# The first block of a mixer in another order, and two residual sums in front of the last running product

## The chip, the cores and the metric

The kernel runs on one NeuronCore of one Trainium2 chip. Its engines each work through a queue of their own: TensorE (PE, matrix products into PSUM), VectorE (DVE), ScalarE (ACT), GpSimd (POOL) and SyncE (SP, which issues DMAs). They wait for one another by counting semaphores. The metric is the device time of one execution in microseconds (us), lower is better.

## The reference

One decoder layer on `x` of 8 x 256 tokens with 256 channels, in three residual steps: a gated state-space mixer, a causal attention with 16 heads on a second input, and a mixture of 8 experts. The change is in the mixer:

```python
x = _lin(x, w1)
x = _depthwise_conv(x, conv_w, conv_b)
x = jax.nn.silu(x)
x_delta = jax.nn.softplus(_lin(x, dl_w, dl_b))
A_t = _lin(x, A_w, A_b)
A_bar = jnp.exp(-x_delta * A_t)
B_x = _lin(x, B_w, B_b)
A_cum = jnp.cumprod(A_bar, axis=1)
h = jnp.cumsum(B_x * A_cum, axis=1)
ssm_out = _lin(h, C_w, C_b) + _lin(x, D_w, D_b)
x_res = jax.nn.silu(_lin(ssm_out, w2))
z = ssm_out * x_res
out = ssm_out + _lin(z, w3)
```

Its input is the layer norm of `x`, and `x + out` goes on to the attention, after another layer norm.

## The kernel before

**Blocks.** `mixer_and_projections` works on four blocks `i` of 512 tokens (NBLK = 4), channels on the 128 partitions in two halves `m` (DC = 2), the hidden 512 channels in four quarters (HC = 4). Every fp32 product is made of three fp32r products: each operand is split into a high part (a copy by ScalarE, `..._high`) and a low part (the difference, by VectorE or GpSimd, `..._low`), and `split_product` (L101) adds high x high, low x high and high x low. Weights are split so too: `high_weights` (ACT L623), `low_weights` (DVE L1040, POOL L554).

**A block's way.** Layer norm to `xn` (L1045 on VectorE for block 0, `normed` on ScalarE, L631, for the others, which needs `off1` from `offset`, DVE L1060), a turn by PE (`turn_x`, L838), `w1`, the convolution (`before_conv` on ScalarE, `conv` on VectorE, L1085 and L1087), tanh and silu (L651, L1092), high and low part of the result, `sh` and `sl` (ACT L657, DVE L1064 in block 0, afterwards POOL L568). PE then makes the chunks `dl`, `A`, `B` for the four quarters in a ring of four PSUM banks. Per quarter ScalarE takes exp (L666), log (L671) and exp (L676), VectorE `dmin` (L1097), `delta` (L1102, L1106), the running product `running` (a scan in two pieces, L1115) and `weighted` (L1122). ScalarE and GpSimd split the result into `gh` and `gl` (L683, L568). `mixed` (PE) multiplies it by C_w, `summed` (L1143) sums along the tokens. The gate and `w3` of block i - 1 run inside block i; `residual` (L1149) adds the product to `x_sb` in place, and the statistics of the next layer norm follow (L1054, then seven small steps L110 to L118, then `power` on GpSimd, L559).

**Other work in a block.** PE makes `keys`, `values` and, two blocks later, `queries` from the second input. `values(i)` waits for both residuals of block i - 1 (`x_out`). `mixed(i, m)` waits for the low part of the keys, `biased_low(i, "K")` on VectorE (L1164), which stands behind the statistics.

**Order.** All queues are written out by hand; nothing is scheduled. Each engine executes its queue in order, so a wait holds all that stands behind it. Constants and the statistics of blocks 1 to 3 for the first layer norm (`st1`) are put into gaps of the first block.

## Time and profile before

| | us |
|---|---|
| median of 3 runs | 716.22 |
| lowest, highest | 714.62, 717.73 |
| the profiled execution | 713.61 |
| its span | 711.8 |
| PE busy | 609.7 (86%) |
| DVE busy | 501.5 (70%) |
| ACT busy | 353.2 (50%) |
| POOL busy | 334.0 (47%) |

The span goes from the first to the last instruction. Shares are averages over stages: the mixer fills about the first 230 us, the attention and the experts the rest. The mean granted clock of TensorE is 0.926 of full speed; it takes two levels, 0.50 (1.2 GHz) and 1.00 (2.4 GHz).

### The profile page before, as it was taken

What the parts mean: (1) busy time and instruction counts of PE and PEld (TensorE: products, weight loads), DVE (VectorE), ACT (ScalarE), POOL (GpSimd) and SP (SyncE); (2) the same over time, 40 slices, a digit from 0 to 9 for tenths busy, and PEclk for the clock granted to TensorE, in tenths of its full rate; (3) what the DMA queues carried; (4) which work ended last, traced back from release to release, by engine and by line L of the source; (5) the groups of instructions that cost most, each with busy time, mean ns of one, the idle gap of its engine ahead of it and who ended that gap; (6) DMA issues with size and microseconds to landing.
All of it is one profiled execution on the core that took longest, in us unless ns stands there. A gap on an engine that the chain in (4) does not pass through costs nothing.

```text
span 711.8 us, 11906 instructions
## 1 busy us (share of the span) xinstructions
PE 609.7 (86%) x4100; PEld 507.7 (71%) x4100; DVE 501.5 (70%) x1066; ACT 353.2 (50%) x685; POOL 334.0 (47%) x322
## 2 busy tenths in 40 slices
PE   3596998998998789889897833999999999999992
PEld 2374877877876555456564522999999999999991
DVE  5777579689679956677776441687787878887740
ACT  4566472672452333354534311566666666666650
POOL 1224624223232003422453375446767868686776
PEclk9898999999999988999999755899999999999997
DMA  9300500873726944865673303505446252621223
GB/s 291 100 1 30 148 29 18 260 242 93 196 63 165 222 93 97 235 152 148 169 198 115 107 26 121 175 6 164 98 101 163 37 174 29 173 30 17 26 32 45
DMA packets 63315, 81.64 MB, mean 115 GB/s; under 512 B 10295, under 2 KB 47938, under 8 KB 63256
## 3 DMA queue, kind: packets, MB, share of 16 engines
q1 hardware_dynamic: 53928, 72.85, 36.4%
q0 software_dynamic: 9216, 7.81, 7.6%
q8 instruction: 33, 0.54, 0.3%
q10 hardware_dynamic: 112, 0.23, 0.1%
q14 instruction: 26, 0.21, 0.1%
HBM read 48.27 MB, written 34.36 MB: 116 GB/s over the span
## 4 chain that ended last, share of the span: by engine, by line
PE 40%; DVE 6%; DMA 5%; POOL 4%; issue 4%; ACT 2%; SPq 1%; POOLq 0%; DVEq 0%; ACTq 0%
PE l_scores L101 14%; PE l_turned L1857 7%; PE l_out L1857 3%; PE l_shared L1857 3%; DMA l_hi<-md 3%; POOL out L1561 2%; PE l_turned L337 2%; PE l_scores L1791 2%; PE l_shared L1733 2%; PE l_out L357 2%; DMA l_lo<-kd 1%; PE l_scores L1814 1%; PE l_turned L321 1%; DVE l_nm L291 1%; POOL disp L1530 1%
## 5 line engine op out<-in xcount | busy, mean ns | idle before, releaser
L2046 DVE SCALAR_TENSOR_TENSOR w_v<-w_th,l_scores 128x324 f32<-128x324 f32 x128 | 62.2, 491 | 56.5 <-ACT w_th L1648 56.0
L1648 ACT ACTIVATE w_th<-l_scores 128x324 f32<-128x324 f32 x128 | 56.5, 441 | 84.1 <-PE l_scores L101 83.3
L1548 POOL TENSOR_TENSOR l_lo<-w_v,l_hi 128x324 fp32r<-128x324 f32 x64 | 59.0, 922 | 75.6 <-ACT l_hi L1654 75.4
L367 ACT ACTIVATE l_area<-l_turned 128x1024 f32<-128x1024 f32 x48 | 49.1, 1023 | 88.6 <-PE l_turned L337 88.4
L101 PE MATMUL l_scores<-l_hi,w_w1h 128*128 128x324 f32 x256 | 81.4, 318 | 2.3 <-DVE l_lo L2038 1.1
L1561 POOL DMA_INDIRECT out<-l_area,w_to x48 | 76.3, 1591 | 12.2 <-issue 10.0
L101 PE MATMUL l_scores<-l_lo,w_w1h 128*128 128x324 f32 x256 | 80.8, 316 | 0.0
L101 PE MATMUL l_scores<-l_hi,w_w1l 128*128 128x324 f32 x256 | 80.7, 315 | 0.0
L291 DVE TENSOR_REDUCE l_nm<-l_scores 128x4 f32<-128x1024 f32 (+1 forms) x45 | 54.8, 1217 | 25.0 <-PE l_scores L277 24.8
L1654 ACT ACTIVATE l_hi<-w_v 128x324 fp32r<-128x324 f32 x128 | 59.9, 472 | 12.4 <-DVE w_v L2046 11.8
L2020 DVE TENSOR_TENSOR w_w2l<-w_s,w_w2h 128x256 fp32r<-128x256 f32 x56 | 60.2, 1075 | 1.9
L1537 POOL TENSOR_TENSOR w_w1l<-w_s,w_w1h 128x256 fp32r<-128x256 f32 x64 | 55.3, 864 | 1.7 <-ACT w_w1h L1633 0.2
L101 PEld LDWEIGHTS l_scores<-l_hi,w_w1h 128*128 128x128 f32 x256 | 49.2, 192 | 3.0 <-ACT l_hi L1643 2.9
L101 PEld LDWEIGHTS l_scores<-l_hi,w_w1l 128*128 128x128 f32 x256 | 49.4, 193 | 0.0
L101 PEld LDWEIGHTS l_scores<-l_lo,w_w1h 128*128 128x128 f32 x256 | 49.3, 193 | 0.0
L101 PE MATMUL l_scores<-m_sh,l_hi 128*128 128x512 f32 x96 | 39.5, 412 | 9.6 <-ACT m_sh L657 6.9
L1520 POOL TENSOR_TENSOR a_on<-a_po,a_rc 128x256 f32<-128x256 f32 x16 | 9.9, 620 | 73.5 <-DVE a_rc L1933 73.5
L568 POOL TENSOR_TENSOR m_gl<-m_acc,m_gh 128x512 fp32r<-128x512 f32 x16 | 24.5, 1533 | 37.4 <-ACT m_gh L683 37.4
L101 PE MATMUL l_scores<-m_sl,l_hi 128*128 128x512 f32 x96 | 38.8, 404 | 0.0
L101 PE MATMUL l_scores<-m_sh,l_lo 128*128 128x512 f32 x96 | 38.7, 403 | 0.0
L559 POOL TENSOR_TENSOR m_rstd<-m_ve,c_mhalf 128x4 f32<-128x4 f32 (+1 forms) x7 | 8.3, 1189 | 63.2 <-DVE m_ve L118 63.2
L1530 POOL DMA_INDIRECT disp<-w_x,w_si x32 | 31.7, 992 | 12.1 <-issue 8.2
(449 smaller groups left out, 1733.2 us busy)
## 6 DMA issues: line engine op xcount, KB each, us to landing
w_s<-in_L_ffn_w SPq DMA_DIRECT2D x14, 1024.0 KB, 6.4
l_lo<-kd SPq DMA_DIRECT2D x32, 200.0 KB
l_hi<-qd SPq DMA_DIRECT2D x32, 192.0 KB
disp<-c_blank SPq DMA_DIRECT2D x8, 658.1 KB
w_rows<-disp SPq DMA_DIRECT2D x7, 658.1 KB
kd<-l_qkh SPq DMA_DIRECT2D x16, 256.0 KB, 4.7
vd<-l_area SPq DMA_DIRECT2D x4, 1024.0 KB, 6.8
qd<-l_qkh SPq DMA_DIRECT2D x16, 256.0 KB, 4.4
```

Of the source, the lines that this page charges most:

```text
L101: mm = pe.matmul(out, a, b, start=first and n == 0, stop=last and n == 3 * len(parts) - 1)
L291: dve.tensor_reduce(dst, src, AX.X, ALU.max).then_inc(A["nm"], 1)
L367: act.activation(lead.pr[n % 3][:, :], lead.tbank[:, :], ACT.Exp, scale=SCALE).then_inc(A["exp"], 1)
L1530: pool.indirect_dma_start(out=disp, out_offset=bass.IndirectOffsetOnAxis(ap=si[:, k, t:t + 1], axis=0), in_=x3[:, t, :], in_offset=None, b ...
L1537: pool.tensor_tensor(w1_piece(w1l, f), w1_piece(s1[e % 2], f), w1_piece(w1h, f).bitcast(F32), ALU.subtract)\
L1548: pool.tensor_tensor(hl[:, g % 3, half(1)], v[:, n % 4, :], hh[:, g % 3, half(1)].bitcast(F32), ALU.subtract)\
L1561: pool.indirect_dma_start(out=out, out_offset=bass.IndirectOffsetOnAxis(ap=to[:, e % 3, t:t + 1], axis=0), in_=y[e % 2][:, t, :], in_offse ...
L1648: act.activation(th[:, n % 2, :], hb[n % 2][:, 0:HALF], ACT.Tanh, scale=0.5).then_inc(F["th"], 1)
L1654: act.activation(hh[:, g % 3, half(u)], v[:, n % 4, :], ACT.Copy).then_inc(F["hh"], 1)
L1857: mm = pe.matmul(eb[2 * k + u][:, 0:HALF], w2_piece(w, f)[:, k * P:(k + 1) * P], a[:, g % 3, half(q)], start=f == 0 and n == 0, stop=f == ...
L2020: dve.tensor_tensor(w2_piece(w2l, f), w2_piece(s2[e % 2], f), w2_piece(w2h, f).bitcast(F32), ALU.subtract)\
L2046: dve.scalar_tensor_tensor(v[:, n % 4, :], th[:, n % 2, :], 1.0, hb[n % 2][:, 0:HALF], ALU.add, ALU.mult).then_inc(F["v"], 1)
```

## The change

It has two parts. In the first block:

- PE makes the four products `dl` and `A` of quarters 0 and 1 together, `first_chunks`: first all that needs channel half 0 of `sh` and `sl`, then half 1. Before, each product was finished in turn and all waited for both halves.
- VectorE does the bn_stats of block 1 (`sums`) ahead of the first convolution, the rest of those statistics between the two convolutions, which are interleaved with silu and low parts, and the statistics of blocks 2 and 3 ahead of the loop (before: inside it).
- ScalarE makes `sh` half by half, takes `normed(1)` ahead of the high parts of D_w, C_w and of WQ to WV, and the latter, as well as those of w2 and w3, later in the loop.
- GpSimd waits for `off1` ahead of its low part of WQ to WV.

In blocks 1 to 3 VectorE does the two residuals ahead of `running(i, 3)` and `weighted(i, 3)`; before, behind them.

```diff
@@ GpSimd @@
                 power(2, ve1, rstd1, slice(TPB, 2 * TPB))
+                pool.wait_ge(S["off1"], 1)
                 low_weights(("WQ", "WV"))
@@ ScalarE @@
                 def direct(i):
+                    if i == 0:
+                        act.wait_ge(S["half"], 3)
...
                 x_tanh(0, 0)
+                s_high(0, 0)
                 x_tanh(0, 1)
+                s_high(0, 1)
+                normed(1)
                 high_weights(("D_w", "C_w"), ("in_CD", 32))
-                s_high(0, 0)
-                s_high(0, 1)
                 act.preload_act_table_set("natural_log_exp_and_others")
-                high_weights(("WQ", "WV"), ("in_att", 48))
-                act.wait_ge(S["half"], 3)
                 for i in range(NBLK):
                     now, last = i < NBLK, 0 <= i - 1 < NBLK
-                    if i + 1 < NBLK:
+                    if 0 < i < NBLK - 1:
                         normed(i + 1)
...
                     if i == 0:
-                        high_weights(("w2", "w3"), ("half", 4))
+                        high_weights(("WQ", "WV"), ("in_att", 48))
                     if last:
                         ssm_high(i - 1, 0)
                     if now:
                         log(i, 1)
                     if i + 1 < NBLK:
                         x_high(i + 1)
+                    if i == 0:
+                        high_weights(("w2", "w3"), ("half", 4))
@@ PE @@
+                def first_chunks():
+                    four = (("dl", 0), ("A", 0), ("dl", 1), ("A", 1))
+                    for name in ("dl", "A"):
+                        split_done(pe, name + "_w")
+                    for k in range(DC):
+                        pe.wait_ge(S["sh"], k + 1)
+                        for name, m in four:
+                            (wh_, wl_), _ = products(name + "_w", m, (sh, sl))[k]
+                            pe.matmul(ring(name, m)[:, :], wh_, sh[:, k, :], start=k == 0, stop=False, skip_group_check=True)
+                            pe.matmul(ring(name, m)[:, :], wl_, sh[:, k, :], start=False, stop=False, skip_group_check=True)
+                        pe.wait_ge(S["sl"], k + 1)
+                        for name, m in four:
+                            (wh_, _), _ = products(name + "_w", m, (sh, sl))[k]
+                            mm = pe.matmul(ring(name, m)[:, :], wh_, sl[:, k, :], start=False, stop=k == DC - 1,
+                                           skip_group_check=True)
+                            if k == DC - 1:
+                                mm.then_inc(S["made"], 1)
@@ VectorE @@
                 low_weights("B_w", "B_w")
+                dve.wait_ge(S["x1"], 16)
+                sums(st1, TPB, 2 * TPB)
                 conv(0, 0)
-                conv(0, 1)
+                variance_and_mean(dve, own, S["ve"], st1, mom1, ve1, slice(TPB, 2 * TPB))
+                conv_first(0, 1)
                 silu(0, 0)
+                conv_last(0, 1)
+                low("sl", sl, cv[:, 0, :], sh, "sh", 0, 1)
                 silu(0, 1)
-                low("sl", sl, cv[:, 0, :], sh, "sh", 0, 1)
                 low("sl", sl, cv[:, 1, :], sh, "sh", 1, 2)
+                offset(2, slice(TPB, 2 * TPB))
+                dve.wait_ge(S["x2"], 16 * (NBLK - 2))
+                statistics(st1, mom1, ve1, 2 * TPB, NT)
                 low_weights("D_w", "C_w")
-                dve.wait_ge(S["x1"], 16)
-                statistics(st1, mom1, ve1, TPB, 2 * TPB)
...
-                offset(2, slice(TPB, 2 * TPB))
                 for i in range(NBLK):
...
                         running(i, 1)
-                    if i == 0:
-                        dve.wait_ge(S["x2"], 16 * (NBLK - 2))
-                        statistics(st1, mom1, ve1, 2 * TPB, NT)
...
                         weighted(i, 2)
+                    if last:
+                        residual(i - 1, 0)
+                        residual(i - 1, 1)
+                    if now:
                         running(i, 3)
                         weighted(i, 3)
                     if last:
-                        residual(i - 1, 0)
-                        residual(i - 1, 1)
                         dve.wait_ge(S["x_out"], 2 * i)
                         statistics(st2, mom2, ve2, TPB * (i - 1), TPB * i)
```

How the queues stand, at three places. ScalarE in the first block, before, from the two tanh (output `l_area`) to the first exponential of softplus (output `m_e`); `m_sh` is the high part, `m_xn` the output of `normed(1)`:

```order
L651 ACTIVATE l_area<-m_cv 128x512 x2
L623 ACTIVATE l_hi<-m_stage 128x1536
L657 ACTIVATE m_sh<-m_cv 128x512 x2
L752 ACT_TABLE_LOAD
L623 ACTIVATE m_wh<-m_stage 128x1536
L631 ACTIVATE m_xn<-g_x,m_off,m_rstd 128x256 x4
L666 ACTIVATE m_e<-l_scores,m_dlb 128x512
```

and now:

```order
L652 ACTIVATE l_area<-m_cv 128x512
L658 ACTIVATE m_sh<-m_cv 128x512
L652 ACTIVATE l_area<-m_cv 128x512
L658 ACTIVATE m_sh<-m_cv 128x512
L632 ACTIVATE m_xn<-g_x,m_off,m_rstd 128x256 x4
L624 ACTIVATE l_hi<-m_stage 128x1536
L756 ACT_TABLE_LOAD
L667 ACTIVATE m_e<-l_scores,m_dlb 128x512
```

The layer norm of block 1 moved in front of the weights, and the 1536-column copy of WQ to WV left this stretch. VectorE in the first block, before, between the low part of B_w and the loop (some rows of the variance left out by cutting at its first step):

```order
L1085 SCALAR_TENSOR_TENSOR m_cv<-m_ypad,m_cw,m_cv 128x512
L1087 SCALAR_TENSOR_TENSOR m_cv<-m_ypad,m_cw,m_cv 128x512
L1085 SCALAR_TENSOR_TENSOR m_cv<-m_ypad,m_cw,m_cv 128x512
L1087 SCALAR_TENSOR_TENSOR m_cv<-m_ypad,m_cw,m_cv 128x512
L1092 SCALAR_TENSOR_TENSOR m_cv<-l_area,m_cv 128x512 x2
L1064 TENSOR_TENSOR m_sl<-m_cv,m_sh 128x512 x2
L1040 TENSOR_TENSOR l_lo<-m_stage,l_hi 128x1536
L1054 BN_STATS m_st<-g_x 128x6 x4
```

and now, from the last step of block 1's variance on:

```order
L118 TENSOR_TENSOR m_ve<-m_mom 128x4
L1112 SCALAR_TENSOR_TENSOR m_cv<-m_ypad,m_cw,m_cv 128x512
L1126 SCALAR_TENSOR_TENSOR m_cv<-l_area,m_cv 128x512
L1121 SCALAR_TENSOR_TENSOR m_cv<-m_ypad,m_cw,m_cv 128x512
L1091 TENSOR_TENSOR m_sl<-m_cv,m_sh 128x512
L1126 SCALAR_TENSOR_TENSOR m_cv<-l_area,m_cv 128x512
L1091 TENSOR_TENSOR m_sl<-m_cv,m_sh 128x512
L1087 SCALAR_TENSOR_TENSOR m_off<-m_mom,m_rstd 128x4
L1078 BN_STATS m_st<-g_x 128x6 x8
```

The two halves are interleaved, and `m_off`, which releases ScalarE's `normed(1)`, follows at once; the eight bn_stats of blocks 2 and 3 stand here now. VectorE at the end of block 1, before (`m_acc` with one input is the running product, `g_x` the residual):

```order
L1122 SCALAR_TENSOR_TENSOR m_acc<-l_scores,m_Bb,m_acc 128x512
L1115 SCALAR_TENSOR_TENSOR m_acc<-m_e 128x256 x2
L1122 SCALAR_TENSOR_TENSOR m_acc<-l_scores,m_Bb,m_acc 128x512
L1149 TENSOR_TENSOR g_x<-l_out,g_x 128x512
L1149 TENSOR_TENSOR g_x<-l_shared,g_x 128x512
L1054 BN_STATS m_st<-g_x 128x6 x4
```

and now:

```order
L1156 SCALAR_TENSOR_TENSOR m_acc<-l_scores,m_Bb,m_acc 128x512
L1183 TENSOR_TENSOR g_x<-l_out,g_x 128x512
L1183 TENSOR_TENSOR g_x<-l_shared,g_x 128x512
L1149 SCALAR_TENSOR_TENSOR m_acc<-m_e 128x256 x2
L1156 SCALAR_TENSOR_TENSOR m_acc<-l_scores,m_Bb,m_acc 128x512
L1078 BN_STATS m_st<-g_x 128x6 x4
```

The residuals changed places with the last running product and its weighting; what is ahead and behind stayed.

## Rows read from the trace of the kernel before

**Rows 1.** Busy time by stage: stretch, its length, busy us of each engine, clock.

```profile
65.00:100.00 35.00, 35.00 (x156) 28.81 (x157) 23.12 (x36) 20.88 (x35) 15.43 (x27) 0.92 0.29 75
```

**Rows 2.** Timeline, 15 to 37 us: start, duration, engine, line, operation, [idle <-releaser].

```profile
20.02 0.75 DVE L1085 SCALAR_TENSOR_TENSOR m_cv<-m_ypad,m_cw,m_cv 128x512 f32<-128x512 f32 x1 [0.93 <-ACT m_cv L646]
...
24.15 1.29 DVE L1064 TENSOR_TENSOR m_sl<-m_cv,m_sh 128x512 fp32r<-128x512 f32 x2 [1.20 <-ACT m_sh L657]
24.66 1.28 ACT L752 ACT_TABLE_LOAD   x1
...
25.95 1.49 ACT L623 ACTIVATE m_wh<-m_stage 128x1536 fp32r<-128x1536 f32 x1
...
29.40 1.20 POOL L559 TENSOR_TENSOR m_rstd<-m_ve,c_mhalf 128x4 f32<-128x4 f32 x1 [20.18 <-DVE m_ve L118]
...
30.57 3.48 POOL L554 TENSOR_TENSOR m_wl<-m_stage,m_wh 128x1536 fp32r<-128x1536 f32 x1
...
30.63 3.44 DVE L1060 SCALAR_TENSOR_TENSOR m_off<-m_mom,m_rstd 128x4 f32<-128x4 f32 x1 [0.90 <-POOL m_rstd L559]
...
34.15 2.07 ACT L631 ACTIVATE m_xn<-g_x,m_off,m_rstd 128x256 f32<-128x256 f32 x4 [6.72 <-issue]
...
36.13 0.67 ACT L666 ACTIVATE m_e<-l_scores,m_dlb 128x512 f32<-128x512 f32 x1
```

**Rows 3.** Timeline of DVE, 36 to 70 us, end of block 0.

```profile
44.47 1.26 DVE L1115 TENSOR_TENSOR_SCAN m_acc<-m_e 128x256 f32<-128x256 f32 x2
...
48.07 2.68 DVE L1054 BATCH_NORM_STATS2 m_st<-g_x 128x6 f32<-128x256 f32 x8
...
53.90 1.65 DVE L1087 SCALAR_TENSOR_TENSOR m_cv<-m_ypad,m_cw,m_cv 128x512 f32<-128x512 f32 x1
...
60.03 2.29 DVE L1115 TENSOR_TENSOR_SCAN m_acc<-m_e 128x256 f32<-128x256 f32 x2
```

**Rows 4.** Timeline of POOL, 26 to 72 us.

```profile
41.27 2.42 POOL L554 TENSOR_TENSOR m_wl<-m_stage,m_wh 128x1024 fp32r<-128x1024 f32 x1 [7.22 <-ACT m_wh L623]
```

**Rows 5.** Timeline of PE, 50 to 66 us.

```profile
64.94 0.77 PE L101 MATMUL l_out<-m_xbh,m_wh 128*128 128x512 f32 x1 [5.54 <-DVE m_xbl L1064]
```

**Rows 6.** Timeline of DVE, 100 to 130 us, end of block 1.

```profile
113.30 1.27 DVE L1115 TENSOR_TENSOR_SCAN m_acc<-m_e 128x256 f32<-128x256 f32 x2
...
115.94 0.68 DVE L1149 TENSOR_TENSOR g_x<-l_shared,g_x 128x512 f32<-128x512 f32 x1
...
118.71 1.24 DVE L112 TENSOR_TENSOR m_mom<-m_st 128x4 f32<-128x4 f32 x1
...
120.41 1.41 DVE L1164 SCALAR_TENSOR_TENSOR l_qkl<-l_turned,m_bk,l_qkh 128x512 fp32r<-128x512 f32 x2
```

**Rows 7.** Timeline of POOL, the same stretch.

```profile
114.00 1.63 POOL L568 TENSOR_TENSOR m_gl<-m_acc,m_gh 128x512 fp32r<-128x512 f32 x1 [5.86 <-ACT m_gh L683]
...
117.41 2.52 POOL L568 TENSOR_TENSOR m_sl<-m_cv,m_sh 128x512 fp32r<-128x512 f32 x2
```

**Rows 8.** Timeline of PE: first product of values(1), first of mixed(1, 0).

```profile
116.68 0.39 PE L101 MATMUL l_out<-m_wh,m_xbh 128*128 128x256 f32 x1 [2.34 <-DVE g_x L1149]
...
121.96 0.47 PE L101 MATMUL l_turned<-m_gh,l_hi 128*128 128x512 f32 x1 [0.94 <-DVE l_qkl L1164]
```

**Rows 9.** Timeline of PE: first product of mixed(3, 0).

```profile
221.03 0.47 PE L101 MATMUL l_turned<-m_gh,l_hi 128*128 128x512 f32 x1 [0.63 <-DVE l_qkl L1164]
```

**Rows 10.** Stretches of PE: length, busy us (matmuls), granted clock, DMA share, GB/s.

```profile
18.70:25.50 6.80, 0.00 (x0) 0.78 0.71 216
25.55:29.30 3.75, 3.75 (x9) 0.50 0.00 0
29.30:33.00 3.70, 3.70 (x16) 0.99 0.00 0
...
64.94:70.20 5.26, 5.26 (x13) 0.50 0.00 0
...
118.20:121.50 3.30, 2.82 (x14) 0.50 0.00 0
```

More of the change, by code:

```diff
@@ L872, in chunk @@
                         pe.wait_ge(S["sl"], DC * (i + 1))
-                    if i == 0 and m == 0:
-                        split_done(pe, name + "_w")
+                    if i == 0 and name == "B" and m == 0:
+                        split_done(pe, "B_w")
                     ge(pe, S["ring"], made(i, name, m) - 4)
                     split_product(pe, ring(name, m)[:, :], products(name + "_w", m, (sh, sl))).then_inc(S["made"], 1)
+                def first_chunks():
[15 more added lines that the diff above has]
+                                mm.then_inc(S["made"], 1)
                 def direct(i):
@@ L970, in _ @@
                     now, last = i < NBLK, 0 <= i - 1 < NBLK
-                    if now:
+                    if i == 0:
+                        first_chunks()
+                    else:
                         chunk(i, "dl", 0)
@@ L975, in _ @@
                         queries(i - 2)
-                    if now:
+                    if i > 0:
                         chunk(i, "dl", 1)
@@ L1050, in last_sum, with sums, statistics @@
                     dve.tensor_tensor(ssm[:, m, :], ssm[:, m, :], dx[:, m, :], ALU.add).then_inc(S["ssm"], 1)
-                def statistics(st, mom, ve, n0, n1):
+                def sums(st, n0, n1):
                     for n in range(n0, n1):
                         own.step(dve.bn_stats(st[:, n, :], tile(n)))
+                def statistics(st, mom, ve, n0, n1):
+                    sums(st, n0, n1)
                     own.settled()
@@ L1080, in last_low, with conv_first @@
                     dve.tensor_tensor(out[:, m, :], src[:, m, :], high[:, m, :].bitcast(F32), ALU.subtract).then_inc(S[name], 1)
-                def conv(i, m):
+                def conv_first(i, m):
                     dve.wait_ge(S["tap"], DC * i + m + 1)
@@ L1085, in conv, with conv_last @@
                     own.step(dve.scalar_tensor_tensor(out, ypad[:, m, :, 0:L], cw[:, m, 0:1], out, ALU.mult, ALU.add))
+                def conv(i, m):
+                    conv_first(i, m)
+                    conv_last(i, m)
+                def conv_last(i, m):
+                    out = cv[:, m, :].rearrange("p (b l) -> p b l", b=2)
                     own.settled()
```

## The prediction

> **What bounds the kernel now.** I read the table of busy time by stage, then the timeline of each engine through the first block and the end of the second, then the clock. The mixer works on four blocks of 512 tokens. From 65 us on PE is busy for the whole of the next 35 us [rows 1]. Before that it waits: its products for the keys of block 0 start at 64.94 us after 5.54 us of idle time, released by VectorE's low part of the context (`c_low`) [rows 5]. So an edit in the first block is worth what it brings that instruction forward; after it PE is full and the lead is kept, since in block 1 the others wait for PE.
>
> In the first block the chain is this. ScalarE reaches `normed(1)` at 34.15 us after 6.72 us of idle time and the first softplus exponential at 36.13 [rows 2]. It waited for VectorE's tiny `offset` (L1060), which took 3.44 us because GpSimd began the 1536-column low part of WQ to WV at 30.57, 0.06 us earlier, and the two ended together at 34.07 and 34.05 [rows 2]. Operations of VectorE with two SBUF inputs stand still beside a GpSimd product: L1087 takes 1.65 instead of the 0.75 of L1085, a pair of scans 2.29 instead of 1.26 [rows 2, 3]. Those with a PSUM input do not.
>
> At the end of blocks 1 to 3 VectorE, not PE, sets the pace. PE waits 2.34 us at `values` for the residuals (L1149) and then 0.94 us at `mixed` for the keys' low parts (L1164) [rows 8]. VectorE goes from running(3) to those low parts without a gap of note [rows 6].
>
> **First block.** `conv(0,1)` now stands between `sums`, the variance and the silu steps. The four bn_stats (half of the eight's 2.68 [rows 3]) fit into VectorE's wait ahead of the convolution. From L1085 at 20.02 [rows 2] seven operations of 128x512 follow one another across VectorE and ScalarE (conv, silu, conv, tanh, silu, high, low), each 0.65 (half of L1064's 1.29) to 0.75: about 4.9 us, so the last low part ends at about 24.95, `offset` at 25.1. Then `normed(1)` 2.07, the high part of D_w and C_w 1.49 (the 1536 columns of L623), the table load 1.28 [rows 2]: the first exponential starts at 30.0 instead of 36.13. The PE order matters little here: 24 products that start at 22.2 instead of 25.55, about nine of them at half clock [rows 10], end near 29.3, before ScalarE asks for them.
>
> One thing takes part of that back. `power(2)` on GpSimd, 1.20 us at 29.40, comes at about 19.95 now, just ahead of the second L1085, which reads two SBUF tiles. I take 0.9 us for it, and nothing to 1.2 as bounds: exponential at 30.9, lead 5.2.
>
> From there to the first scan (44.47 [rows 3]) the order is kept, except that the copy of WQ to WV (1.49) now stands where w2 and w3 did (1024 columns; two thirds of it): 0.45 us more. VectorE asks for the scan at about 39.7. GpSimd, which before did its 3.48 us piece in the old wait, now runs it from about 36.5 to 40.0, and the 2.42 us piece [rows 4] follows at once; the pair of scans straddles both and ends near 43.5 instead of 45.73. Lead: 2.2. Without the hold it would be 4.8.
>
> The statistics of blocks 2 and 3 leave their place between running(0,1) and delta(0,2): from 48.07 to 51.61, 3.5 us, on VectorE's path and with no cover [rows 3]. Their new place lies under the table load and `normed(1)` of ScalarE. The GpSimd low part that held L1087 for 0.9 us [rows 3] will now hold the scan pair instead, 1.03 us: a wash. Sum: 2.2 + 3.5 - 0.1 = 5.6 us; I take **5.5**. Upper bound 9.1: neither `power` (0.9) nor the two weight pieces (2.6) hold VectorE. Lower bound 4.5: `power(3)` gets in as well.
>
> **Residuals ahead of running(3).** In block 1 the residuals now run at 113.2 to 114.5, and `values` start 2.3 us earlier. That wait goes. But the keys' low parts stay behind the same set of VectorE operations, and PE must have them for `mixed`. So what is late next is L1164, and nothing is gained: PE only waits further down. Then the shift costs:
>
> Scan. At 113.30 it began ahead of GpSimd's `g_low(1,2)` (114.00) and ended at 114.57; GpSimd paid (1.63 instead of 1.26) [rows 6, 7]. Asked for at 114.5, it finds GpSimd in the middle until about 115.3: the pair ends at 116.55 where 115.8 was due, 0.75 us.
>
> Variance. weighted(3) ends 2.0 us later than before (1.27 for the residuals, 0.75), so `g_low(1,3)` and the two `s_low` run from 118.1 to 121.9 instead of 116.2 to 119.9 [rows 7]. L112 already loses about 1.1 us to them: it takes 1.24 for four columns [rows 6]. Of the seven small steps now one more falls on a GpSimd product: L115 and L118 read two SBUF inputs each, and the second `s_low` lasts until 121.9. No row shows L115 held; the nearest is L1060, same form and size, held for 3.44 [rows 2]. I take it: 1.25 us. Not held, the cost would be 0.15.
>
> So the low parts end at 123.8, not 121.82 [rows 6]: **2.0** us per block, 0.9 at the least. In block 3 there is no `s_low`; scan 0.75 and one held step 0.6 give 1.35 on the 221.03 of [rows 9].
>
> The Trainium skill, "SBUF — State Buffer", section "Who interferes with whom", says that a VectorE instruction with two SBUF inputs contends with a GpSimd one that reads SBUF, and that whichever issues first keeps the port for its whole length. By that rule L115 is held, and the 2.0 stands; by the row of L112 alone it would be 0.9. The trace agrees with the rule at L1060 and L1087.
>
> Clock. PE's two waits become one: `values` end at about 117.4 and `mixed` starts at 123.8, 6.4 us. After the idle stretch up to 25.5 us [rows 10] and the 5.54 us of [rows 5] PE ran for 3.75 and 5.26 us at 0.50 of its clock (1.2 GHz) [rows 10], at nine products where it does sixteen. Today the slow stretch (118.20 to 121.50 [rows 10]) falls on `values` with a wait behind it and costs nothing; then it falls on `mixed`, with none. Half of 3.75 is 1.9 us per block, 2.6 at most, 0 at least. In block 3 the gap is about 3.3 us; 0.8.
>
> Sum of this part: 2 x (2.0 + 1.9) + 1.35 + 0.8 = **10.0 us lost**. Ends: 2.3 (the scan alone, three times 0.75) and 12.3 (2 x 4.6 + 1.35 + 1.7).
>
> **Total.** -5.5 + 10.0 = +4.5 us. The profiled execution took 713.61 (span 711.8), 2.6 below the median of 716.22; against it the sum is 718.1, against the median, which I forecast, **720.7**.
>
> **Rivals.** (a) *The first block wins.* The mechanism is that VectorE's order at the end of a block does no harm: GpSimd's pieces fall between the small steps, and `values` running straight behind the keys keep the clock high. Then the second part costs 0 to 2.3 and the first brings 5.5 to 9: 716.2 - 6 = 710. For it: the waits of PE at `values` (2.34 [rows 8]) do go. Against: L1164 comes after the same VectorE work in either order. It decides at a clock of 1.00 in `mixed` and a start of it no later than today, counted from the block's first `c_low`. Chance 0.22.
>
> (b) *Even.* The first block brings 7 to 8 (the scan gets in ahead of the 2.42 us piece), the second costs 6 to 8 (L115 not held, slow stretch half under the wait): 715 to 717. For it: both holds are matters of 0.1 us in arrival. Chance 0.30.
>
> (c) *My forecast*, both holds and the slow clock: 720 to 724. Chance 0.48.
>
> (d) That the change does not do what it says: the 3.44 us hold cannot come back, since GpSimd now waits for `off1`; I give it nothing.
>
> **Numbers.** The ends are 716.2 - 9.1 + 2.3 = 709.4 and 716.2 - 4.5 + 12.3 = 724.0; with about a microsecond of scatter between executions above, and the unlikely corner of two bounds below left out, the range is 710.5 to 725.0. A measurement of this kernel tells about 0.5% (3.6 us) from no change: faster 0.22, same 0.30, slower 0.48.
>
> **What will show it.** Right, if the first exponential starts near 31 us, `keys(0)` near 59.5, the wait at `values` is gone in blocks 1 to 3, the wait ahead of `mixed` is 4 to 6.5 us and the clock row behind it reads 0.50. Each term has its row: L112 to L118 over more than 2.5 us, the scan of running(3) at about 2.0 in place of 1.27. The forecast is wrong if `mixed(1,0)` starts less than 57.5 us after `keys(0)` (121.96 - 64.94 = 57.02 today), or if `keys(0)` starts before 57 us.

## The result, and the profile after

The changed kernel takes 723.70 us (median of 4 runs, 720.85 to 725.75), the kernel before, run beside it on the same chip, 715.42 us (4 runs). The ratio is 1.0099 with a 95% interval of 1.0056 to 1.0142: slower by about one per cent. (Ratios here leave disturbed executions out, so a ratio and the quotient of two medians can differ a little.) The profiled execution took 722.88 us with a span of 721.2, where that of before had 713.61 and 711.8.

The first block did gain what the prediction wanted of it. These are rows of the timeline of ScalarE and of VectorE of the changed kernel; the first two answer to [rows 2], the scan to [rows 3]:

```profile
24.49 2.08 ACT L632 ACTIVATE m_xn<-g_x,m_off,m_rstd 128x256 f32<-128x256 f32 x4 [0.83 <-DVE m_off L1087]
...
29.67 0.69 ACT L667 ACTIVATE m_e<-l_scores,m_dlb 128x512 f32<-128x512 f32 x1 [0.42 <-PE l_scores L895]
...
38.45 3.69 DVE L1149 TENSOR_TENSOR_SCAN m_acc<-m_e 128x256 f32<-128x256 f32 x2
```

`normed(1)` starts at 24.49 instead of 34.15, the first exponential at 29.67 instead of 36.13, and the first pair of scans ends at 42.14 (38.45 + 3.69) instead of 45.73. The whole way of the change is best read from PE, cut where a block's first `mixed` product starts, up to the first product of the attention (L321) and to the last of its output projection. The stretches of PE in the kernel before (length, busy us and matmuls, granted clock, DMA share, GB/s):

```profile
0.00:64.94 64.94, 36.73 (x133) 0.91 0.37 116
64.94:121.96 57.02, 52.94 (x260) 0.92 0.21 56
121.96:174.55 52.59, 48.82 (x244) 0.97 0.67 198
174.55:221.03 46.48, 43.91 (x224) 1.00 0.51 126
221.03:248.52 27.49, 22.61 (x140) 0.99 0.90 222
248.52:411.51 162.99, 141.86 (x1350) 0.90 0.55 144
```

and in the changed one:

```profile
0.00:57.97 57.97, 35.42 (x133) 0.92 0.41 130
57.97:115.96 57.99, 51.10 (x261) 0.94 0.20 55
115.96:171.94 55.98, 49.10 (x245) 0.96 0.64 186
171.94:222.21 50.27, 46.41 (x225) 0.94 0.48 116
222.21:251.24 29.03, 24.13 (x141) 0.91 0.89 218
251.24:421.65 170.41, 149.89 (x1350) 0.85 0.52 137
```

Line by line: 6.97 us won up to `keys(0)`, then 0.97, 3.39, 3.79 and 1.54 lost (9.69), so the attention starts 2.7 us later than before. From there to the output projection another 7.4 us are lost, at a clock of 0.85 instead of 0.90, with the same 1350 matmuls and not an instruction changed. The prediction has no term for that last part. It is most of the measured difference, and it is a question of its own below.

What the change did at the end of block 1 shows on three engines. VectorE (answers to [rows 6]):

```profile
106.17 0.68 DVE L1183 TENSOR_TENSOR g_x<-l_shared,g_x 128x512 f32<-128x512 f32 x1
106.77 2.05 DVE L1149 TENSOR_TENSOR_SCAN m_acc<-m_e 128x256 f32<-128x256 f32 x2
...
111.70 1.23 DVE L112 TENSOR_TENSOR m_mom<-m_st 128x4 f32<-128x4 f32 x1
112.96 1.19 DVE L114 TENSOR_SCALAR m_mom<-m_mom 128x4 f32<-128x4 f32 x1
...
114.41 1.40 DVE L1198 SCALAR_TENSOR_TENSOR l_qkl<-l_turned,m_bk,l_qkh 128x512 fp32r<-128x512 f32 x2
```

GpSimd (answers to [rows 7]) and PE (answers to [rows 8]):

```profile
106.40 1.29 POOL L568 TENSOR_TENSOR m_gl<-m_acc,m_gh 128x512 fp32r<-128x512 f32 x1 [5.86 <-ACT m_gh L684]
...
111.64 2.49 POOL L568 TENSOR_TENSOR m_sl<-m_cv,m_sh 128x512 fp32r<-128x512 f32 x2
```

```profile
106.90 0.39 PE L101 MATMUL l_out<-m_wh,m_xbh 128*128 128x256 f32 x1 [0.16 <-DVE g_x L1183]
...
115.96 0.77 PE L101 MATMUL l_turned<-m_gh,l_hi 128*128 128x512 f32 x1 [5.94 <-DVE l_qkl L1198]
```

The scan pair waits for the rest of `g_low(1, 2)` (106.40 to 107.69) and takes 2.05 instead of 1.27. Two of the seven small steps stand still beside the `s_low` pair (111.64 to 114.13), where one did before. And the two waits of PE, 2.34 at `values` and 0.94 at `mixed`, are now 0.16 and 5.94, after which `mixed` runs at half clock. The last shows in two stretches, the first 3.94 us of `mixed` and the 2.00 us behind:

```profile
115.96:119.90 3.94, 3.94 (x9) 0.50 0.68 147
119.90:121.90 2.00, 2.00 (x14) 0.98 0.95 238
```

Nine products in 3.94 us, then fourteen in 2.00. Blocks 2 and 3 have the wait ahead of `mixed` too, 5.93 and 3.08 us.

### The profile page after: what moved, and what is told of

The parts are those of the page before. It is cut to its first block, busy times and chain, and to the rows that moved or that the text cites. A ratio compares the mean times of both kernels' runs of the same rounds, so it can differ in the third digit from the quotient of the medians.

```text
span 721.2 us, 11908 instructions
## 1 busy us (share of the span) xinstructions
PE 618.1 (86%) x4100; PEld 512.2 (71%) x4100; DVE 505.7 (70%) x1066; ACT 353.1 (49%) x685; POOL 333.7 (46%) x322
## 3 DMA queue, kind: packets, MB, share of 16 engines
q1 hardware_dynamic: 53928, 72.85, 36.2%
## 4 chain that ended last, share of the span: by engine, by line
PE 43%; issue 5%; DVE 5%; POOL 3%; DMA 3%; ACT 2%; SPq 1%; POOLq 0%; DVEq 0%; ACTq 0%
PE l_scores L101 14%; PE l_turned L1894 7%; PE l_out L1894 4%; PE l_shared L1894 3%; PE l_out L357 2%; PE l_turned L337 2%; PE l_turned L321 2%; PE l_scores L1828 2%; PE l_shared L1770 2%; PE l_scores L1851 1%; PE l_scores L277 1%; DMA l_lo<-kd 1%; PE l_scores L262 1%; POOL out L1598 1%; POOL disp L1567 1%
## 5 line engine op out<-in xcount | busy, mean ns | idle before, releaser
L101 PE MATMUL l_scores<-m_sh,l_hi 128*128 128x512 f32 x88 | 35.6, 405 | 2.3 <-DVE m_e L1136 1.6
L1149 DVE TENSOR_TENSOR_SCAN m_acc<-m_e 128x256 f32<-128x256 f32 x32 | 37.1, 1199 | 0.0
L1894 PE MATMUL l_turned<-l_hi,w_w2h 128*128 128x324 f32 x128 | 33.8, 335 | 2.2 <-DVE w_yt L2095 1.3
L101 PE MATMUL l_scores<-m_sh,l_lo 128*128 128x512 f32 x88 | 34.9, 396 | 0.0
```

What stands on the lines that cost most here:

```text
L101: mm = pe.matmul(out, a, b, start=first and n == 0, stop=last and n == 3 * len(parts) - 1)
L1894: mm = pe.matmul(eb[2 * k + u][:, 0:HALF], w2_piece(w, f)[:, k * P:(k + 1) * P], a[:, g % 3, half(q)], start=f == 0 and n == 0, stop=f == ...
```

## The experiments

The theory (A) is the prediction's: the reordered first block wins some 6 us, moving the residuals loses more, since the keys' low parts (L1198, before L1164) stay behind the same VectorE work and PE's merged wait brings half clock upon `mixed`. The rivals: (B) the first block itself costs something further on; (C) the holds between VectorE and GpSimd are the price, the clock is not; (D) the loss lies in the attention and has nothing to do with the wait. Where a clock is turned into time, "slow us" is the length of a stretch times (1 - clock) times 2, that is how long PE stood at 1.2 GHz.

One table for all runs. "Attention at" is where the first attention product (L321) starts in the trace, minus the 248.52 of before: the mixer's whole account. "Median" is the difference of the medians against the kernel before on the same chip. "Attention" is the length of the stretch that follows, 162.99 in the trace of before.

| kernel | attention at | median | ratio (95%) | attention |
|---|---|---|---|---|
| the change | +2.7 | +8.3 | 1.0099 (1.0056 to 1.0142) | 170.4 |
| the change, again | +0.6 | +3.1 | 1.0025 (0.9998 to 1.0052) | 167.7 |
| first block only | -3.9 | -6.3 | 0.9923 (0.9893 to 0.9953) | 164.6 |
| residuals only | +7.3 | +11.4 | 1.0215 (1.0163 to 1.0267) | 163.3 |
| the change, wait filled | -3.7 | -3.6 | 0.9986 (0.9949 to 1.0023) | 165.8 |
| the change, keys before variance | -3.9 | -2.9 | 0.9995 (0.9957 to 1.0033) | 162.7 |
| the change, `power` early | -1.6 | -1.2 | 0.9987 (0.9946 to 1.0027) | 172.4 |
| first block, keys early | -6.7 | -1.7 | 0.9938 (0.9904 to 0.9971) | 171.7 |
| the same, both `mixed` together | -7.8 | -9.8 | 0.9880 (0.9842 to 0.9919) | 161.5 |
| the same, again | -10.6 | -10.5 | 0.9870 (0.9811 to 0.9929) | 164.9 |
| the same, residuals early | -4.4 | -3.7 | 0.9938 (0.9895 to 0.9980) | 171.8 |
| the same, `power` early too | -4.2 | -4.7 | 0.9940 (0.9899 to 0.9981) | 160.6 |
| both `mixed` together, `values` wait filled | -9.7 | -8.3 | 0.9904 (0.9863 to 0.9945) | 170.1 |

Except in three rows (the change, the residuals only, and the first block with keys early: 5.6, 4.1 and 5.0 us), the mixer's account and the median agree within 2.6 us.

The median is of all executions, the other two columns are of the one that was traced. That one was the shortest of its kernel for the residuals only and for keys before variance, and the longest for the first block only, for `power` early, and for "the same, residuals early". So the last column doesn't rank the kernels. Each execution's mean granted clock is known as well, and says more:

| kernel | executions | clock, lowest | median | highest |
|---|---|---|---|---|
| the change, both measurements | 16 | 0.900 | 0.914 | 0.926 |
| first block only | 11 | 0.920 | 0.928 | 0.932 |
| residuals only | 6 | 0.897 | 0.907 | 0.924 |
| first block, keys early | 12 | 0.913 | 0.918 | 0.927 |
| both `mixed` together, both measurements | 10 | 0.929 | 0.932 | 0.937 |

### The first block alone

From the changed kernel, VectorE's loop:

```diff
-                    if last:
-                        residual(i - 1, 0)
-                        residual(i - 1, 1)
-                    if now:
                         running(i, 3)
                         weighted(i, 3)
                     if last:
+                        residual(i - 1, 0)
+                        residual(i - 1, 1)
```

> The first part of the change alone; the residuals stand behind weighted(3) again. Theory: the lead of 7.0 us that the trace of the changed kernel shows at keys(0) (57.97 against 64.94) is kept to the end, since PE is full afterwards: about 708.5 against 715.4, mixed(1,0) 57.0 after keys(0) with waits of 2.3 and 0.9 us on PE. Rival: the extra 6.7 us that the changed kernel loses behind the mixer (in the attention) come with the first part, by the shift of everything in time; then this kernel is within 2 us of the kernel before.

Measured: 708.74 us (11 runs, 705.79 to 711.02), ratio 0.9923. The first half of the change is a gain of 6.3 us, and theory A's number is met, but not its reason: in the trace (of the longest of the eleven executions) the lead is not kept to the end. Rival B isn't quite dead, then. The trace shows PE ahead of `values(1)` and of `mixed(1, 0)`:

```profile
109.79 0.39 PE L101 MATMUL l_out<-m_wh,m_xbh 128*128 128x256 f32 x1 [2.35 <-DVE g_x L1183]
...
115.10 0.76 PE L101 MATMUL l_turned<-m_gh,l_hi 128*128 128x512 f32 x1 [2.19 <-DVE l_qkl L1198]
```

In [rows 8] the second product lasted 0.47 us and its wait was 0.94; here it is 0.76 and 2.19, because the half-clock stretch, which in the trace of before lay over `values` with a wait behind it, now lies over `mixed`. (The wait is longer because `values` ran at full clock and were done sooner; `mixed` starts only 0.17 us later after `keys(0)`.) So of the 7.0 us that `keys(0)` leads (57.91 instead of 64.94), 3.1 are gone when the attention starts. VectorE's order in this block is that of before. That today's slow stretch costs nothing was a property of where it happened to fall in one execution.

### The residuals alone

From the kernel before:

```diff
-                        running(i, 3)
-                        weighted(i, 3)
                     if last:
                         residual(i - 1, 0)
                         residual(i - 1, 1)
+                    if now:
+                        running(i, 3)
+                        weighted(i, 3)
+                    if last:
                         dve.wait_ge(S["x_out"], 2 * i)
```

> The second part alone: the kernel before with the two residuals ahead of running(3). Theory: it carries the loss: 9.7 us up to the end of the mixer (1.0 + 3.4 + 3.8 + 1.5 in the trace of the changed kernel), so about 725, and 731 if the 6.7 us in the attention belong to it as well; PE waits about 6 us ahead of mixed(1,0) and mixed(2,0) and runs it at a clock of 0.50. Rival: the residuals only expose a loss that the first part makes (its lead cannot be kept); then this kernel is within 2 us of 715.4.

Measured: 726.45 us (6 runs, 720.07 to 733.63), ratio 1.0215. The wait moved just as described:

```profile
114.16 0.39 PE L101 MATMUL l_out<-m_wh,m_xbh 128*128 128x256 f32 x1 [0.15 <-DVE g_x L1149]
...
123.22 0.77 PE L101 MATMUL l_turned<-m_gh,l_hi 128*128 128x512 f32 x1 [5.94 <-DVE l_qkl L1164]
```

The mixer's account is +7.3 us (9.7 were expected), the median +11.4. The trace is of the shortest of the six executions, at a mean clock of 0.924; the other five had 0.897 to 0.915, so its attention of 163.3 us isn't typical of this kernel. The two halves of the change add up, -6.3 + 11.4 = +5.1, which lies between the two measurements of the whole, +8.3 and +3.1.

### The merged wait filled with products

The changed kernel; PE makes products into a free bank after `values` until the keys are due, as many as fit. Nothing reads them, and they are no part of what is computed.

```diff
                         values(i)
+                        if i:
+                            pe.wait_ge(S["ring"], 12 * i + 9)
+                            for _ in range(12 if i == NBLK - 1 else 22):
+                                pe.matmul(banks[0], c["identr"][:, :], high_part(columns("WQ")), start=True, stop=True)
                         mixed(i, 0)
```

> The changed kernel with 22 spare products of 512 columns on PE between values(i) and mixed(i,0) in blocks 1 and 2, 12 in block 3 (5.1 and 2.8 us, less than the waits of 5.9 and 3.1 us); they write a free PSUM bank and nothing reads them. They keep PE at work and change no wait. Theory: mixed(1,0) and mixed(2,0) start when they did but run at a granted clock of 1.00: about 2 us less in each of the two blocks, 1 us or less in the third, so about 718.5 against 723.7 and mixed(1,0) to mixed(2,0) 54.2 us instead of 56.0. Rival: the low clock costs nothing, because VectorE or ScalarE set the pace behind mixed; then 723 to 724, or more by what the products take.

Measured: 711.50 us (10 runs, 709.81 to 724.78), ratio 0.9986. The order of VectorE and GpSimd is untouched, and `mixed(1, 0)` starts no earlier (57.86 us after `keys(0)`, with the residue of a wait). Only the clock differs:

```profile
115.49:119.50 4.01, 4.01 (x22) 1.00 0.68 148
...
115.49:169.80 54.31, 52.48 (x267) 1.00 0.64 192
```

22 products in the 4.01 us in which the changed kernel made nine. From `mixed(1)` to `mixed(2)` it is 54.31 us; the two traces of the changed kernel have 55.98 and 56.31. Over the four stretches of the mixer behind `keys(0)` it is 187.2 us instead of 193.3 and 191.1. So the clock is worth 4 to 6 us in the mixer, less or more by the scatter between executions: rival C falls, and the prediction's clock terms (2 x 1.9 + 0.8 = 4.6 us) are of the right size. The median gained 7 to 12 us, more than expected; the rest isn't in the mixer.

### The keys' low parts before the small steps

The changed kernel; VectorE:

```diff
-                        statistics(st2, mom2, ve2, TPB * (i - 1), TPB * i)
+                        sums(st2, TPB * (i - 1), TPB * i)
                     if now:
                         biased_low(i, "K", bk, i)
                     if last:
+                        own.settled()
+                        variance_and_mean(dve, own, S["ve"], st2, mom2, ve2, slice(TPB * (i - 1), TPB * i))
+                    if last:
                         normed(i - 1)
```

> The changed kernel with the keys' low parts moved from behind the variance to between the bn_stats and the seven small steps. Theory (PE waits for L1164, not for the residuals): L1164 ends about 3.4 us earlier in blocks 1 and 2, mixed(i,0) starts 3 us earlier and PE's wait shrinks from 5.9 to about 2.5 us; turn_q then waits up to 2 us for the normed rows, whose statistics stay where they are, so 1.5 to 3 us are won per block, in all 4 to 8: 716 to 720. Rival (the wait is only renamed, the variance and what follows sets the pace): within 1.5 us of 723.7.

Measured: 712.12 us (10 runs, 708.25 to 720.86), ratio 0.9995. The wait ahead of `mixed` shrinks by the 3.5 us of the seven small steps:

```profile
112.02 0.47 PE L101 MATMUL l_turned<-m_gh,l_hi 128*128 128x512 f32 x1 [2.48 <-DVE l_qkl L1198]
...
118.14 0.66 PE L842 MATMUL l_out<-c_ident,m_xn 128*128 128x128 f32 x4 [1.53 <-DVE l_area L1208]
```

and the first `mixed` product takes 0.47 us, full clock. A new wait of 1.53 us appears at `turn_q` (L842), which needs the layer norm that now comes later. The kernel is 4 to 8 us below its forecast of 716 to 720. Part of that is the attention, the shortest but two of all (162.7 us).

### The change once more

The identical program once more, measured with more executions.

> The changed kernel once more, unchanged, with more executions and another trace. In its first trace the attention (first turned score product to the last output product) takes 170.4 us, in five other traces of five kernels 162.7 to 165.8, with 51 us against 26 to 40 us of PE at half clock. Theory A (that stretch at half clock came with that one execution): here it takes 162 to 166 us, and the median falls to about 719 to 722, since the two parts measured alone give -6.3 and +11.4. Theory B (it follows from the order in the mixer): again about 170 us, and the median stays at 723.7.

Measured: 718.66 us (12 runs, 712.61 to 726.72) against 715.54 (29 runs), ratio 1.0025. The waits ahead of `mixed` are the same to 0.01 us (5.93, 5.94, 3.08). The stretches behind `keys(0)` measure 58.46, 56.31, 48.83 and 27.49: 7.5 us more than before, not 9.7. The attention is again long. That stretch in four kernels, first this one, then both `mixed` together, the first block with keys early, and the first block alone:

```profile
249.07:416.78 167.71, 149.01 (x1351) 0.85 0.53 140
```

```profile
240.75:402.21 161.46, 140.13 (x1350) 0.91 0.55 145
```

```profile
241.86:413.57 171.71, 151.59 (x1351) 0.84 0.52 136
```

```profile
244.61:409.19 164.58, 143.42 (x1350) 0.89 0.55 143
```

With 0.91 the stretch takes 161 us, with 0.84 it takes 172. In slow us these are 50.3, 29.1, 54.9 and 36.2; the kernel before has 32.6 and the changed one 51.1. So the same 1350 matmuls, the same code, cost up to 11 us more or less with the time that PE stands at half clock.

### `power` ahead of the `s_low` pair

The changed kernel; GpSimd:

```diff
+                    if last:
+                        power(3 + i, ve2, rstd2, slice(TPB * (i - 1), TPB * i))
                     if i + 1 < NBLK:
                         s_low(i + 1, 0)
                         s_low(i + 1, 1)
-                    if last:
-                        power(3 + i, ve2, rstd2, slice(TPB * (i - 1), TPB * i))
```

> The changed kernel with GpSimd's power of the second layer norm ahead of the two low parts s_low(i+1) in blocks 1 and 2, so that these no longer run beside the small steps of the variance. Theory (GpSimd's products hold VectorE's steps with two SBUF inputs or fast single inputs): L112 and L114 fall from 1.23 and 1.19 us to 0.17, only L110 is still held by g_low(3), L1198 ends 2.2 us earlier, mixed(1,0) starts 2 us earlier (PE's wait 5.9 to about 3.7), and the kernel wins 4 to 6 us: about 718. Rival (the long small steps are the profiler's or VectorE's own): steps stay long, and s_low, now later by 3 us, makes no difference or costs: 723 to 725.

Measured: 714.31 us (10 runs, 709.48 to 719.82), ratio 0.9987; the changed kernel beside it took 718.66, so 4.3 us are won, as expected, from a lower start. This is the hold by itself: with GpSimd waiting for the variance, there is no `s_low` to run into.

```profile
111.78 0.15 DVE L112 TENSOR_TENSOR m_mom<-m_st 128x4 f32<-128x4 f32 x1
111.97 0.17 DVE L114 TENSOR_SCALAR m_mom<-m_mom 128x4 f32<-128x4 f32 x1
...
112.39 1.40 DVE L1198 SCALAR_TENSOR_TENSOR l_qkl<-l_turned,m_bk,l_qkh 128x512 fp32r<-128x512 f32 x2
113.71 3.19 DVE L1190 TENSOR_SCALAR m_xn<-g_x,m_mom,m_rstd 128x256 f32<-128x256 f32 x4
```

L112 takes 0.15 instead of 1.23, L114 0.17 instead of 1.19: 2.1 us in all, and the wait ahead of `mixed(1, 0)` is 3.85 instead of 5.94. The hold has only moved, though: the layer norm (L1190), 1.38 us in the changed kernel, now meets the `s_low` pair and takes 3.19. Nobody waits for it at once. L114 has a single input, in SBUF, and was held all the same. The Trainium skill, "SBUF — State Buffer", section "Who interferes with whom", counts `tensor_scalar` in its fast modes among what can contend with GpSimd; the rows of L114 (1.0 us longer) and of L1190 (1.8 us longer) agree.

### Keys early, without the residuals

The first block alone, with VectorE's edit of the keys as above.

> The first part of the change alone, with the keys' low parts between the bn_stats and the small steps. In the first part alone PE waits 2.3 us at values and 2.2 us at mixed(1,0). Theory: the wait at values stays (the residuals stand where they did), the wait at mixed falls away (low parts 2.4 us earlier), turn_q waits up to 2 us instead: 0 to 1.5 us per block, 705 to 708 against 708.7. Rival: nothing is won because turn_q's wait takes all: 708 to 709.

Measured: 713.84 us (12 runs, 705.61 to 717.22), ratio 0.9938. A miss: 6 us above the upper end expected. The mixer did what it should (attention at -6.7 us), but the attention of this trace took 171.7 us, and the median shows something of the kind. By the mixer alone this version had to beat the first block alone, by 2.8 us; by its median it doesn't.

### Both `mixed` in a row

The kernel above; PE:

```diff
                         mixed(i, 0)
+                        mixed(i, 1)
                     if last:
                         turn_q(i - 1)
-                    if now:
-                        mixed(i, 1)
```

> As e5, and PE makes both halves of mixed before it turns the rows for the queries (turn_q). Theory: the wait of turn_q for the normed rows is covered by the second half of mixed (2.8 us), so both waits behind values are gone: 703 to 706. Rival: what follows turn_q (x2_high, x2_low, the queries two blocks on) is on the path, and its delay of 2.8 us costs what is won: 707 to 709.

> e6 once more (first part of the change, keys' low parts early, both halves of mixed ahead of turn_q), for an interval beside e12 on one chip: its four executions gave 703.1 to 708.2. Expected 705 to 708; the start of the attention to its last output product varies between executions by up to 10 us with the share at half clock, so a median above 709 would say that the four were lucky draws.

Measured: 705.70 us (4 runs, 703.14 to 708.23), ratio 0.9880, and once more, on another chip, 704.24 us (6 runs, 700.56 to 707.25), ratio 0.9870. The first is as expected, the second 0.8 us below the range. The twelve products of the second half cover the time in which VectorE makes the variance and the layer norm, so that neither `turn_q` nor `mixed` waits; the wait for the residuals remains:

```profile
109.70 0.39 PE L101 MATMUL l_out<-m_wh,m_xbh 128*128 128x256 f32 x1 [2.32 <-DVE g_x L1182]
```

This is the fastest version of the study, and beats both the kernel before and the changed one.

The two medians are 8.1 and 9.6 us below the one of the first block with keys early, and the mixer's account explains only 1.1 and 3.9 of that. The rest lies behind the mixer. The clocks say the same: 0.929 to 0.937 in these ten executions, 0.913 to 0.927 in those twelve, and the two ranges don't touch. Outside the attention the three traces have about 60 slow us each; in it they have 54.9, 29.1 and 36.3. So by these executions an edit in the mixer changes how long PE stands at half clock in the attention, whose instructions are the same. By which step it does so, no run shows.

### The residuals early, in this better order

The changed kernel with both edits; then with `power` early too.

> Both parts of the change, with the keys' low parts between the bn_stats and the small steps and both halves of mixed ahead of turn_q: e6 with the residuals ahead of running(3). Theory: in e6 PE waits 2.3 us at values in blocks 1 and 2 and nowhere behind it; here the wait at values is 0.15 us, but mixed then waits about 2.5 us for the keys' low parts and gl(3), which stand 0.8 us later than in e6 because the scan is held by GpSimd. So even with the low parts early, moving the residuals wins nothing: e6 plus 1 to 5 us, 707 to 711. Rival: with the low parts out of the way the residuals' move pays what it promised, 2.3 us in two blocks: e6 minus 2 to 5, 701 to 704.

> As e12, and GpSimd's power ahead of s_low(i+1). Theory: the rows for the queries are normed about 1 us earlier, which both halves of mixed already cover, and s_low holds VectorE elsewhere (its four normed rows took 3.19 instead of 1.38 us in e9): within 2 us of e12. Rival: the lock at the small steps is still on the path: 3 us or more below e12.

Measured: 711.10 us (12 runs, 705.38 to 717.14), ratio 0.9938, and 710.05 us (12 runs, 705.10 to 713.86), ratio 0.9940. The profiled execution of the first was itself the longest of its twelve, so of its trace the mixer is what counts:

```profile
113.32 0.47 PE L101 MATMUL l_turned<-m_gh,l_hi 128*128 128x512 f32 x1 [2.49 <-DVE l_qkl L1197]
```

Even here the residuals ahead of `running(3)` only move the wait: 2.49 us at `mixed` instead of 2.32 at `values`. Both are 4 to 7 us above the version with the residuals behind. `power` early changes nothing once the keys no longer stand behind the small steps: the attention starts at 244.31 with it and at 244.17 without.

### The wait at `values` filled

Both `mixed` together, with 9, 9 and 4 products that nothing reads ahead of `values` in blocks 1 to 3.

> e6 (the fastest so far, 704 to 706) with 9 spare products of 512 columns between keys(i) and values(i) in blocks 1 and 2 and 4 in block 3: 2.1 and 0.9 us, less than the waits of 2.3 and 1.1 us. Theory (a wait of PE costs more by the half clock behind it than by itself): the stretches of half clock after values go, 3.2 to 4 us of them in the trace of e6 between keys(0) and mixed(2), half of that is won: 702 to 704. Rival: the spare products only fill time that was free, and the half clock in the mixer was rare already: 704 to 706.

Measured: 707.57 us (9 runs, 704.0 to 713.5), ratio 0.9904. A miss: 702 to 704 were expected, and even the rival's 704 to 706 is passed. No gain: the first stretch behind `keys(0)` is the shortest of all (53.97), but the attention starts at -9.7, within the -7.8 and -10.6 of the two traces without the filling. The remaining wait of 2.3 us isn't what costs here.

## Why the prediction was right, and where it wasn't

The direction holds, and the mechanism in the mixer: 720.7 us were forecast for the likeliest case, 4.5 above the median of before (716.2 at the time); measured were 723.7 and 718.7, 8.3 and 3.1 above the kernel before beside them. Its last paragraph named two signs of a wrong forecast, and neither came: `mixed(1, 0)` starts 57.99 us after `keys(0)` (less than 57.5 would have been one), and `keys(0)` at 57.97 (before 57). But that the sum comes out near is in part luck. The mixer, all that it was added up from, lost 2.7 and 0.6 us in the two traces and not 4.5, since the first block won 7.0 and not 5.5 and the second part took 9.7 and 7.5 and not 10.0; the attention, which has no term, added 7.4 and 4.7.

**First exponential**, forecast 30.9, measured 29.67. The term of 0.9 us for a hold of the convolution by `power` failed. VectorE and GpSimd in that place:

```profile
19.52 0.16 DVE L118 TENSOR_TENSOR m_ve<-m_mom 128x4 f32<-128x4 f32 x1
19.60 0.74 DVE L1112 SCALAR_TENSOR_TENSOR m_cv<-m_ypad,m_cw,m_cv 128x512 f32<-128x512 f32 x1
```

```profile
19.76 1.45 POOL L559 TENSOR_TENSOR m_rstd<-m_ve,c_mhalf 128x4 f32<-128x4 f32 x1 [10.72 <-DVE m_ve L118]
```

`power` is released by L118, and L1112 is the next in VectorE's own queue. It started 0.16 us sooner than `power`. VectorE was first and kept its 0.74; GpSimd paid (1.45 instead of 1.20 [rows 2]). I could have read that order beforehand: in the trace of before VectorE's next two operations behind that L118 started at 29.24 and 29.31, and `power` [rows 2] only at 29.40.

**First scan**, forecast 43.5, measured 42.14 (38.45 + 3.69). GpSimd's two weight pieces ran back to back as predicted, from 35.33 for 6.26 us, and the pair of scans stood across them:

```profile
35.33 6.26 POOL L554 TENSOR_TENSOR m_wl<-m_stage,m_wh 128x1536 fp32r<-128x1536 f32 x2 [14.12 <-ACT m_wh L624]
41.55 2.02 POOL L559 TENSOR_TENSOR m_rstd<-m_ve,c_mhalf 128x8 f32<-128x8 f32 x1
```

The hold is there with 2.4 us (3.69 instead of 1.26); everything is 1.2 us earlier by the exponential. So the lead of `keys(0)` is 6.97 and not 5.5; the missing 1.5 are about the `power` term and what follows from it. The prediction's upper bound of 9.1 still needed both holds gone. Its premise that this lead is kept, since PE is full afterwards, did not hold: with the first block alone 3.9 of 7.0 us were left at the attention.

**Scan of running(1, 3)**, forecast +0.75, measured +0.78 (2.05 against 1.27).

**Variance**, forecast 1.25 longer, measured 1.08: from the start of L110 to the end of L118 it is 3.47 us (111.02 to 114.49) instead of 2.39. The instruction is another than I named: L115 (0.15) and L118 (0.16) weren't held; L114 was (1.19), which I had left out because it reads only one tile. So "by that rule L115 is held" was the wrong instruction for a size that came out near.

**Start of the keys' low parts**, forecast 2.0 later per block, measured 0.97 in block 1: 114.41 - 57.97 = 56.44 after `keys(0)` against 55.47 (120.41 - 64.94 of [rows 6, 5]). `weighted(1, 2)`, the last operation ahead of the edit, is in the timeline of VectorE of before and then of the changed kernel:

```profile
112.52 0.74 DVE L1122 SCALAR_TENSOR_TENSOR m_acc<-l_scores,m_Bb,m_acc 128x512 f32<-128x512 f32 x1
```

```profile
104.91 0.74 DVE L1156 SCALAR_TENSOR_TENSOR m_acc<-l_scores,m_Bb,m_acc 128x512 f32<-128x512 f32 x1
```

From it to the keys' low parts are 7.89 us before and 9.50 now: 1.61 later, near to the forecast's 2.0. But it starts 47.58 us after `keys(0)` before and 46.94 now, 0.64 sooner, which no step of the prediction had.

**Clock**, forecast 1.9 per block (0.8 in block 3), and a wait of 6.4 (3.3 in block 3). Measured: waits of 5.94, 5.93 and 3.08, a stretch of 3.94 us with nine products at 0.50, and 4 to 6 us for the mixer when the wait was filled. Right. The sentence beside it, that the slow stretch costs nothing today, is no property of the old order: in the first block alone, with that order of VectorE, the slow stretch lay on `mixed` and took part in 3.1 us of loss.

**The sum of the second part.** By stretches the prediction gives +2.0, +3.9, +3.25 and +0.8: in the second its clock term and the next delay, in the third the clock and the 1.35 of block 3. The changed kernel shows 0.97, 3.39, 3.79 and 1.54, and its repetition 1.44, 3.72, 2.35 and 0.00: 9.7 and 7.5 in place of 10.0. The residuals' own share is smaller, since the first block alone already shows +3.1: 6.6 and 4.4 against that kernel, 7.5 (191.04 - 183.58) in the kernel with the residuals only.

**The attention** was not in the sum, by its silence at nothing. In the traces it added 7.4 and 4.7 us. Where PE stood at half clock is told by the clock's row of 40 slices of the span, of before and then of the changed kernel:

```profile
PEclk9898999999999988999999755899999999999997
```

```profile
PEclk9898998998999976997989755899999999999997
```

Slices 15 and 16 (18 us each) are 7 and 6 in place of 8 and 8, and slice 19 is 7 in place of 9. Is that the doing of the change? In part it is chance. The stretch was 170.4 and 167.7 in the changed kernel, 161.5 and 164.9 in one and the same fast kernel, 171.8 (the longest of twelve executions) and 160.6 in two kernels whose mixers agree to 0.1 us. In part it goes with the arrangement, as the executions' clocks show: 0.900 to 0.926 with the change, 0.920 to 0.932 with its first part alone, 0.897 to 0.924 with the residuals only. The slow stretches in the mixer, told above, are only part of that difference, and the three rows in which the mixer's account and the median disagree by 4 to 6 us all err to the slow side. What in the mixer's order brings the slow attention stays open, and with it the 3 us of the first measurement beyond the sum.

**The rivals.** "The first block wins" was to decide at a clock of 1.00 in `mixed` and at a start of it no later than before; both signs came out against it (0.50, 57.99 against 57.02). "Even" named 715 to 717 and a first block of 7 to 8 with a second part of 6 to 8. In its mixer the repetition fits this rival's terms (7.0 won, 7.5 lost, and L115 not held); only its median, 718.7 us, is above them, between that and the forecast, and taken alone it can't be told from no change; the first measurement, the kernel with the residuals only, and the sum of the halves are on the forecast's side.

## What to carry to other kernels

When an operation is pulled forward to end a wait, look for the last thing that the waiting engine needs before its next long stretch of work, and ask whether that came forward too; if not, the wait goes there, and one wait of 6 us cost more than two of 2.3 and 0.9: what was needed last came later still, beside GpSimd's products, and PE then ran 4 us at half clock with no wait behind to hide it. The repair was to leave the residuals where they were, to pull forward what is needed last (the keys' low parts) and to give PE independent products in the gap (both `mixed` together): 1.2 to 1.3% faster than before, where the change was 0.3 to 1% slower. And price the clock by more than one trace: a stretch at half clock that is hidden in one execution lies on the path in the next.

## What the runs showed of the hardware

- The same attention stretch, with 1350 or 1351 matmuls in the trace, took from 160.6 to 172.4 us in 14 traces, at mean clocks between 0.92 and 0.84. That is 1.6% of the span, above most of the effects under study. It differs between executions of one program (161.5 and 164.9), and with the order of instructions far ahead of it.
- A tiny operation can be held as long as a large one: four columns of L112 and L114 took 1.23 and 1.19 us beside GpSimd's low parts, 0.15 and 0.17 without them. L114 reads one tile only.
- A pair of scans that met two back-to-back GpSimd products (6.26 us) took 3.69 us. Beside one product it took 1.27 to 2.33, by who came first: 1.27 where the product started 0.7 us after the pair's start (60.74 and 60.04 in the changed kernel; the product then took 1.65 itself), 2.33 where it started 0.2 us after it (84.73 and 84.51) and so ahead of the second scan, 2.05 where it was under way.
- Products that nothing reads, put into a wait of 6 us, made the products behind it run 22 in 4.01 us instead of nine in 3.94; the kernel got faster by doing more. In a wait of 2.3 us the same brought nothing.
